# A transformer tower on one core: the last expert layer on chosen pairs, with its weights packed per expert, and clearing issued during the retention heads

## The reference, cut to what matters

```
h = xf @ shared_w1 + shared_b1                     # shared expert, 128 -> 2*96
z = swiglu5(h, *shared_act) @ shared_w2 + shared_b2
gate_probs = softmax(xf @ gate_w + gate_b)
w, idx = top_k(gate_probs, 2); w = w / sum(w); cw = sum(one_hot(idx, 16) * w)
he = einsum('nd,edh->enh', xf, expert_w1) + expert_b1     # all 16 experts
te = swiglu5(he, *expert_act)                      # gate: even columns, up: odd ones
oe = einsum('enh,ehd->end', te, expert_w2) + expert_b2
return einsum('ne,end->nd', cw, oe) + z
# swiglu5: g = clip(gate, +-gc), u = clip(up, +-uc); g * sigmoid(g*alpha) * scale * (u + shift)
```

## Time and profile before

| what | value |
|---|---|
| time, median of 3 runs | 1781.22 us (1778.82 to 2319.34) |
| the profiled execution: its own time, its span | 1777.7 us, 1776.0 us |
| PE, DVE, ACT, POOL busy, share of the span | 79%, 71%, 46%, 47% |
| granted TensorE clock, mean | 0.893 of full |
| retention heads | 158 to 436 us |
| first expert layer | 436 to 637 us |
| last expert layer | 1522 to 1770 us |

### The profile page before, as it was taken

One profiled execution on the slowest core, in us unless ns is written; L12 is line 12 of the kernel. 1 busy time (PEld: TensorE's weight loads), 2 busy tenths in 40 slices (PEclk: granted clock), 3 DMA queues, 4 the chain that ended last, 5 costly groups with the idle time before them and its releaser, 6 DMA issues. The chain is left out here.

```text
span 1776.0 us, 28718 instructions
## 1 busy us (share of the span) xinstructions
PE 1410.2 (79%) x9268; PEld 1001.8 (56%) x9268; DVE 1255.7 (71%) x2420; ACT 809.9 (46%) x1022; POOL 827.8 (47%) x625
## 2 busy tenths in 40 slices
PE   1777999997249721448999999999999996499997
PEld 1544788787249710234566666666666664355554
DVE  5266444431535539645799999999999994579997
ACT  2233434332025310013567666666666661166664
POOL 2024134130166656312355555555556542169997
PEclk9788999999569865557999999999999998699998
DMA  3000000001338500000000000000000000000000
GB/s 112 1 1 1 1 2 2 1 1 38 79 101 231 159 16 0 0 0 1 1 1 1 0 0 0 0 0 0 0 0 0 0 1 1 2 17 11 12 13 29
DMA packets 45848, 37.07 MB, mean 21 GB/s; under 512 B 10988, under 2 KB 37255, under 8 KB 45511
## 3 DMA queue, kind: packets, MB, share of 16 engines
q1 hardware_dynamic: 35990, 28.28, 5.7%
q0 software_dynamic: 2048, 4.20, 0.8%
q10 hardware_dynamic: 7728, 3.55, 0.7%
HBM read 26.83 MB, written 9.18 MB: 20 GB/s over the span
## 5 line engine op out<-in xcount | busy, mean ns | idle before, releaser
L1922 POOL TENSOR_TENSOR ta_ex<-ta_ex,ta_left 128x1024 f32<-128x1024 f32 x128 | 302.3, 2361 | 317.4 <-ACT ta_left L1875 316.7
L1834 PEld LDWEIGHTS ta_ps_o<-ta_exT,ta_vseq 128*32 128x32 f32 x2048 | 213.2, 110 | 101.9 <-ACT ta_exT L1867 88.2
L1785 PE MATMUL ta_ps_s<-ta_kT,ta_qz 128*128 (+1 forms) x512 | 242.5, 596 | 20.8 <-ACT ta_ex L1863 20.0
L1834 PE MATMUL ta_ps_o<-ta_exT,ta_vseq 128*32 128x128 f32 x2048 | 247.6, 274 | 6.4 <-ACT ta_exT L1867 6.4
L1867 ACT ACTIVATE ta_exT<-ta_ps_t 128x1024 f32<-128x1024 f32 x128 | 131.1, 1024 | 145.6 <-PE ta_ps_t L1814 145.6
L1940 DVE MAX8 ta_top<-ta_ps_s 128x8 f32<-128x1024 f32 x128 | 156.7, 1224 | 46.7 <-PE ta_ps_s L1785 46.7
L1947 DVE MATCH_REPLACE8 ta_left<-ta_top,ta_ps_s 128x1024 f32<-128x1024 f32 x128 | 155.3, 1213 | 0.0
L1952 DVE MAX8 ta_top<-ta_left 128x8 f32<-128x1024 f32 x128 | 154.7, 1208 | 0.0
L1957 DVE MATCH_REPLACE8 ta_left<-ta_top,ta_left 128x1024 f32<-128x1024 f32 x128 | 154.6, 1208 | 0.0
L1863 ACT ACTIVATE ta_ex<-ta_ps_s,ta_ntop 128x1024 f32<-128x1024 f32 x128 | 142.1, 1110 | 20.9 <-DVE ta_left L1947 20.1
L1875 ACT ACTIVATE ta_left<-ta_left,ta_ntop 128x1024 f32<-128x1024 f32 x128 | 147.0, 1148 | 1.4
(11 more groups left out here) (568 smaller groups left out, 2503.8 us busy)
## 6 DMA issues: line engine op xcount, KB each, us to landing
l1e_w<-in_L_ffn_W_dram SPq DMA_DIRECT2D x46, 256.0 KB
l1f_rows<-l1f_zero SPq DMA_DIRECT2D x2, 1472.0 KB, 9.4
l1e_x<-l1f_rows SPq DMA_DIRECT2D x46, 64.0 KB, 3.7
l1e_outs<-l1e_y ACTq DMA_DIRECT2D x46, 64.0 KB
l3e_w<-in_L_ffn_expert_w_dram SPq DMA_DIRECT2D x16, 96.0 KB, 1.9
ids<-in_x_dram SPq DMA_DIRECT2D x1, 1024.0 KB
consts<-in_consts_dram SPq DMA_DIRECT2D x1, 1024.0 KB, 5.0
out_dram<-h SPq DMA_DIRECT2D x1, 1024.0 KB, 5.1
```

The lines of the kernel that those rows point to most:

```text
L1785: ins = pe.matmul(ps_s[:, i % 2, half * BANK:(half + 1) * BANK], qz[:, odd, h, :], kT[:, grp, bass.ds(at.key0[i // PAIR] + half * BANK, BA ...
L1834: ins = pe.matmul(ps_o[a:a + 2 * TW, grp * P:(grp + 1) * P], vseq[:, j, h, :], exT[:, i % 2, j, :], start=(j == 0), stop=(j == CH - 1))
L1922: pool.tensor_tensor(ex[:, i % 4, :], ex[:, i % 4, :], left[:, i % 4, :], ALU.subtract).then_inc(kept, 1)
```

## The change

- Last layer: shared expert on all 16 tiles as eight pairs of tiles (`SHARED`), then 64 blocks of 128 chosen rows (32 per sequence, `L3_BLOCKS`) as 32 pairs, with slots as in the first expert layer. Eight stages of weights (`STAGES`), three slots for values between the products (`LAG`).
- One transfer per block brings both weights from a DRAM tensor `l3f_packed`, in which each expert has 128 rows of 320 values; it is written during the heads.
- Biases, clamps, shifts and alphas per block come from products: a table per parameter ([17, 96]) times a matrix of ones where block and owner meet ([17, 65]).
- Clip reads PSUM, adds the bias and takes the upper limit in one DVE operation, the lower limit of the gate in a second; the lower limit of up is taken with the last product on DVE. POOL makes one product per pair and issues scatters and gathers between.
- The clears of both layers and the first layer's small loads are issued by SP in the heads' block; W2 and the last layer's small loads in a layernorm's block. The two blocks that held them are gone.

```diff
-        with nc.Block() as block:
...
-                for b in range(B):
-                    sp.dma_start(r.rows_dram[b].rearrange("(n p) d -> p n d", p=P), zero...).then_inc(r.s_cleared, 16)
...
-        layernorm(nc, m, "ln_l1f", m.h, m.xn, None)
+        layernorm(nc, m, "ln_l1f", m.h, m.xn, None, fetch=fetch)   # fetch: all of W2
...
+        early = [l1_ffn_early(nc, m, w), l3_early(nc, m, w)]
+        l1_heads(nc, m, r, issue_early)                            # block.sync(early)
...
+def l3_early(nc, m, w):
+    def issue(sp):
+        sp.dma_start(m.packed_dram[:, :, 0:2 * L3_I], w["L3_ffn_expert_w1"]).then_inc(m.s_packed, 16)
+        sp.dma_start(m.packed_dram[:, 0:L3_I, 2 * L3_I:], w["L3_ffn_expert_w2"]).then_inc(m.s_packed, 16)
+        sp.dma_start(m.packed_dram[:, L3_I:P, 2 * L3_I:]..., zeros).then_inc(m.s_packed, 16)
+        for b in range(B):
+            sp.dma_start(m.l3_rows_dram[b]..., zeros [P, L3_BLOCKS, D]).then_inc(m.s_l3clear, 16)
...
+        layernorm(nc, m, "ln_l3f", m.h, m.xn, m.xnT, fetch=fetch)  # fetch: 8 small loads
         router(nc, m, r, "l3r", L3_E, r.gate_w[:, :], 1)           # now keeps both picks
         l3_expert_scalars(nc, m, r)
+        slots(nc, m, r, "l3k", L3_E, L3_BLOCKS, r.raw_act[:, 0:L3_E, 1])
...
+    SHARED, PAIRS = TILES // 2, TILES // 2 + B * NB // 2           # 8, 40
+    STAGES, LAG = 8, 3
...
+            def load(j):                                            # SP
+                for n in blocks(j):
+                    s, e = n % STAGES, sp.value_load(r.owner[0:1, n // NB, n % NB:n % NB + 1], ...)
+                    if n >= STAGES:
+                        sp.wait_ge(down_ready, SHARED + (n - STAGES) // 2 + 1)
+                    sp.dma_start(packed[:, s, :], m.packed_dram[bass.ds(e, 1), :, :]...).then_inc(staged[s], 16)
+            def rows(j):
+                if n == 0: sp.wait_ge(scattered[b], 16 * 2 * CH)
+                if q >= 4: sp.wait_ge(x_turned, q - 3)
+                sp.dma_start(x[:, q % 4, :, :], r.rows_dram[b]...)
...
+            for j in range(SHARED, PAIRS):
+                if j + 3 < PAIRS:
+                    rows(j + 3)
+                    load(j + 3)
...
+            for j in range(SHARED):                                 # POOL
+                if j < 4:
+                    for t, k in jobs[4 * j:4 * j + 4]:
+                        scatter(0, t, k)
+                swish(j)
+            for j in range(SHARED, SHARED + NB // 2):
+                swish(j)
+                for t, k in jobs[3 * (j - SHARED) // 2:3 * (j - SHARED + 1) // 2]:
+                    scatter(1, t, k)
+            for j in range(SHARED + NB // 2, PAIRS):
+                swish(j)
+                i = j - SHARED - NB // 2 - 3                        # gather(0, ..), five in four pairs
...
+            for t, k in jobs:
+                gather(1, t, k)
...
+            for j in range(PAIRS):                                  # PE
+                if j + 3 < PAIRS:
+                    up(j + 3)        # waits staged[n % STAGES] before each block's two products
+                down(j)              # waits te_ready
+                if SHARED <= j + 4 < PAIRS:
+                    turn(j + 4)
...
+            for j in range(PAIRS):                                  # ACT
+                sigmoid(j)
+                if SHARED <= j + 3 < PAIRS:
+                    flip(j + 3)
+                if j - 1 >= SHARED:
+                    keep(j - 1)      # copies ps_d out and issues the store
...
+            for j in range(PAIRS):                                  # DVE
+                if j + 2 < PAIRS:
+                    clip(j + 2)      # 4 operations from PSUM, 2 in SBUF
+                hidden(j)            # 2 operations, te = max(up, low) * sig
+                if 1 <= j and j - 1 < SHARED:
+                    add(j - 1)       # shared: h += ps_d * scale
+            ...                      # then combine: 2 operations per tile, after the gathers
```

More of the change, by code:

```diff
@@ L118, with layernorm @@
 L1_BLOCKS = 23
-def layernorm(nc, m, name, src, dst, dstT, gain=None, shift=None, loaded=None):
+L3_BLOCKS = 32
+def layernorm(nc, m, name, src, dst, dstT, gain=None, shift=None, loaded=None, fetch=None):
     with ExitStack() as ctx:
@@ L162, in _ @@
                 pool.tensor_tensor(rstd[:, of], small[:, 4, of], m.neghalf[:, of], ALU.pow).then_inc(rstd_ready, 1)
+        if fetch is not None:
+            block.sync(fetch)
         if dstT is None:
@@ new lines, in l3_experts, with blocks, weights @@
+        gates_turned, gates_in, bias_ready, bias_added, h_step = (
+            sem(k) for k in ("gates_turned", "gates_in", "bias_ready", "bias_added", "h_step"))
+        block = ctx.enter_context(nc.Block())
+        def blocks(j):
+            return [2 * (j - SHARED) + k for k in range(2)]
+        def weights(j, k):
+            n = B * NB if j < SHARED else blocks(j)[k]
+            scalars = [par[:, x, n:n + 1] for x in range(7)]
+            if j < SHARED:
+                return w1_all[:, :], w2_all[:, :], scalars
+            return packed[:, n % STAGES, 0:2 * L3_I], packed[0:L3_I, n % STAGES, 2 * L3_I:], scalars
@@ new lines, in up @@
+            def up(j):
+                q = j - SHARED
+                if j == 0:
+                    pe.wait_ge(shared_in, 32)
+                if q >= 0:
+                    pe.wait_ge(xT_ready, q + 1)
+                if j >= 2:
+                    pe.wait_ge(raised, j - 1)
+                for k in range(2):
+                    if q >= 0:
+                        n = blocks(j)[k]
+                        pe.wait_ge(staged[n % STAGES], 16 * (n // STAGES + 1))
+                    rows = r.hT[:, (2 * j + k) * P:(2 * j + k + 1) * P] if q < 0 else xT[:, q % 2, k * P:(k + 1) * P]
+                    for kind in range(2):
+                        ins = pe.matmul(ps_h[0:L3_I, j % 2, (2 * k + kind) * P:(2 * k + kind + 1) * P], weights(j, k)[0][:, kind::2], rows,
+                                        start=True, stop=True)
+                ins.then_inc(up_ready, 1)
@@ new lines, in combine @@
+            def combine(b, t):
+                hh = m.h[:, b * CH + t, :]
+                for k in range(2):
+                    dve.scalar_tensor_tensor(hh, back[:, b, t, k, :], r.share[:, k, b * CH + t:b * CH + t + 1], hh,
+                                             ALU.mult, ALU.add).then_inc(h_step, 1)
+                    dve.wait_ge(h_step, 2 * (b * CH + t) + k + 1)
+            dve.tensor_copy(mine[:, 0:B * NB], r.owner[0:G, :, :].rearrange("g b n -> g (b n)"))
+            dve.memset(mine[:, B * NB:], float(E)).then_inc(hot_step, 1)
```

445 lines of the change are left out of this document (245 added, 200 removed).

## The result

| | before | after |
|---|---|---|
| time, median | 1781.39 us (1778.82 to 2319.34, 4 runs) | 1808.14 us (1807.04 to 1812.13, 4 runs) |
| ratio, with its 95% interval | | 1.0157 [1.0139, 1.0175] |
| span of the profiled execution | 1776.0 us | 1806.4 us |
| granted TensorE clock, mean | 0.893 | 0.845 |

The forecast was 1768, with a range up to 1796. The kernel is 1.6% slower, outside the range. The one execution of 2319.34 us was in a slow state and does not enter the ratio. I read the profile after in the same order as before. Lines of the page of the changed kernel: the clock by slices, the DMA share, the chain that ended last, the group of the routed up products, and the packed transfer's landing.

What follows compares the result with a forecast made beforehand. POOL was taken to pace the last expert layer, with DVE full too. Terms -17.6 + 9.6 + (212.6 - 216.1) = -11.5 us gave 1766.2 from the profiled execution, 1769.7 from the median; forecast 1768, range 1738 to 1796.

Steps and rivals of the forecast that it cites:

- Part 1: First expert layer's entry: clears, loads and packing moved under the heads, 17.6 us less (bounds 0 and -17.6).
- Part 2: Last layer before it can route: router copies, scalars, slot computation, less a shorter layernorm entry; +9.6 us (bounds 7 and 13).
- Part 3: New expert block up to the first routed down product's end: 45 us after the block's start (bounds 38 and 53).
- Part 4: Last layer's routed loop: weight load's whole latency once per pair, 4.9 us (bounds 4.3 and 6.2), 28 pairs, 137.2 us.
- rival 2: Routed loop: gaps keep PE at the low clock, period 5.65 us, 21 us more, 1789; chance 0.20.
- the landing of the second transfer: Routed loop: a pair's second weight transfer, 160 KB, lands in 2.2 us (bounds 1.9 and 3.7).
- the ring: Routed loop's cycle per pair: SP wake, issue, register read, landing, products; 4.67 us at the high clock, 5.65 at the low.
- The last three pairs: End of the routed loop, pairs with no load behind them: 3.9 us.
- The tail: Last layer, from last down product's end to last combine's end, 16 gathers behind one another: 26.0 us.
- Rival 1: Routed loop: loads come in time, DVE and POOL set about 2.5 us per pair, 1701; chance 0.10.
- Rival 3: Routed loop: transfers land as in the first layer, 3.7 us instead of 2.2, 42 us more, 1810; chance 0.07.
- rival 4: Heads: the clearing does not hide, slowing the heads or coming late; 17.6 us back, 1786; chance 0.04.

Runs made afterwards that it cites:

- e9_part1: Kernel before with only the first expert layer's part: small loads and clears beside the heads, W2 load beside the layernorm; 1764.09 us.
- e6_undo: Changed kernel with the early transfers (small loads, both clears, packing) put back into a block of their own behind the heads; 1837.58 us.
- e5_fill: Changed kernel with seven unused products put into PE's queue ahead of each up product that waits for a load; 1785.83 us.
- e2_both: Changed kernel with both owners of a pair read into registers before SP waits for the down product; 1785.02 us.
- e12_swap_hidden: Changed kernel with down(j) ahead of up(j+3) on PE and hidden(j) ahead of clip(j+2) on DVE, still eight stages; 1730.34 us.
- e8_ahead: Changed kernel with 12 stages, loads five pairs ahead, both owners read first, six row buffers, turns one pair earlier into three buffers; 1721.18 us.
- e1_deep: Changed kernel with 12 weight stages in place of 8 and loads issued five pairs ahead in place of three; 1765.6 us.

## Why the prediction was wrong

By its own terms, on the profiled executions: the forecast was 1776.0 - 11.5 = 1764.5 for the span, measured 1806.4, so 41.9 us were missed.

- **Part 1, right.** -17.6 for the entry: alone it measured some 16 (e9_part1), and hiding costs nothing (e6_undo against the changed kernel). The bound of 0 wasn't needed.
- **Part 2, nearly right.** The slot computation took 11.2 us, 11.5 with its block's entry (forecast 10.6 and 11.0). The expert block starts 3.4 us later than forecast: 1.3 are there at the first layernorm already, 0.5 are the slots, and 1.1 are the last layer's router products, which take 7.01 us where they took 5.94.
- **Part 3, 3.5 us low.** The first routed down product ends 49.0 us after the block's start, not 45.5 (so in the forecast's sum; its text says 45); inside the bounds. The last scatter of the first sequence is out at 30, as forecast (29), so POOL was right. DVE was the short term: shared pairs lie 3.3 us apart, where I had 3.0, as a PSUM clip takes 0.40 us and not "near 0.3".
- **Part 4, the step that failed: "Taking one period in four at the low clock gives 4.9".** Nearly all periods ran at the low clock (0.50 to 0.57 in the stretches from 1620 on). By the forecast's own price that is 0.75 us more in each, 21 us. e5_fill shows the clock's share by itself: 0.9 us per period at equal waits. The mechanism was named, as rival 2, with 1789, and was given 0.20; the row that I leaned on against it shows a stretch of 4 us with 2.05 busy at 1.00, in which the clock may simply not have fallen yet, as its second row, 0.85, lets one suspect. "So the high clock should hold once it is there" did not follow from it. In the changed kernel the clock is 0.97 before the first wait for a load and 0.53 in the next 21 us with PE busy for 11.9. The better row was the one at the end of the old stage, at the low clock with gaps in PE, and I had it.
- **Part 4, a second term, the landing of the second transfer.** The sum took 2.2 us from the second issue's start, and 0.05 to the products. That is right for the first transfer of a pair (2.33 to the products), but the second one, which is in the ring, takes 2.63, 0.38 more. The page's median of 2.2 hides this, since most landings that the trace has are of first transfers. Why the second is slower was not tested; SP issues the load of the rows 0.4 us behind it, and in e2_both, too, it is the slower one. The register read and the products took 0.05 less each. The 28 periods took 166.4 us, 5.94 each and not 5.65: 8.2 us more. So rival 2 too, rightly summed, gives 1797.
- **The last three pairs** took 7.6 us, not 3.9: with no more up products beside them, each down product waits for sigmoid, swish and `te` of its own pair.
- **The tail** was 26.0 us, as forecast; between the last combine and the end of the span stand 7.9 us instead of 5.8.

Sum: 3.4 + 3.5 + 21.0 + 8.2 + 3.7 + 0 + 2.1 = 41.9.

What was right is the mechanism: the load's latency once per pair, PE's two waits for packed transfers, down products queued behind. The runs that take it out (e12_swap_hidden, e8_ahead) gain 78 and 87 us, a part of it by the clock, which rises with it. Rival 1 (1701, 2.5 us per pair) was right about what DVE would bound if the loads were in time. Rival 3 is out as it was put, with 2.2 and 2.6 us instead of 3.7, though a small part of it is the second transfer; rival 4 is out, as the clears hid.

## What to carry to other kernels

When a loop waits on a transfer once per turn, write the ring down with every link, with each transfer of the turn priced for itself, and price it at the low clock: here the gaps that the ring makes in PE kept the clock low (0.50, and 0.96 when they were filled), so "mostly high" isn't a middle value but a case that has to be earned. A buffer's refill should hang on something two turns back; before adding buffers, look whether the order written on each engine eats the lead that there is: here two exchanged calls, one on PE and one on DVE, were worth 78 us, and the one on PE alone 6, within the scatter. When a wait goes away, look for what stood behind it (a turn just before its use, an operation behind another's wait), since the first fix often brings only the next link to light.

## What the runs showed of the hardware that I had not expected

- The clock did not follow PE's busy time alone. Over the same 60 us, e1_deep shows 45.8 us busy at a granted 0.53, and e8_ahead 42.4 us busy at 0.94. At the low clock a product's time is double, so a high busy share can come from the clock itself; the two stretches hold 193 and 289 records.
- Useless products can pay: seven per pair gave 22 us back in this loop, which waits for loads (e5_fill).
- Two equal transfers issued 1.1 us apart, with another behind them, did not land alike: 2.33 us from issue to products for the first, 2.63 for the second (the changed kernel).
- Issuing large strided transfers held SP: 5.26 us for the packing of the first weights, 3.9 for each clear of 2 MB (e6_undo). What was issued before counts too: the same load of W2 took 6.09 us there and 0.82 in the changed kernel. Beside the heads they cost nothing; in front of the stage they were its start.
